# List tiles of a routed FFN: weights fetched per tile from DRAM into fixed buffers, the bias as one matmul, result addresses on VectorE

## The chip, the cores and the metric

One Trainium2 chip, one core of it. The metric is the device time of one execution in microseconds; a run's time is somewhat longer than the span that its profile covers. On this core TensorE (PE) multiplies, VectorE (DVE) and ScalarE (ACT) work on SBUF and PSUM, GpSimd (POOL) works on SBUF and issues indirect DMAs, and SyncE (SP) issues the plain ones.

## The reference

`x` is 4 batches of 512 tokens of width 128 (2048 tokens). Four residual blocks follow one another, each on a layer-normalised `x`: causal attention with 16 heads of 8 and rotary positions, a routed FFN, a gated scan with a convolution of three taps, and the same routed FFN again. The FFN, which the change is about, cut to its core:

```python
scores = sigmoid(xf @ Wg.T + bg + bias)                  # 8 experts
top_scores, top_idx = top_k(scores, 2)                   # two per token
weights = zeros(T, E).at[arange(T)[:, None], top_idx].add(top_scores)
h = gelu(einsum('td,ehd->teh', xf, W1) + b1)             # hidden 512
eo = einsum('teh,edh->ted', h, W2) + b2
combined = einsum('ted,te->td', eo, weights)
shared = gelu(xf @ Ws1.T + bs1) @ Ws2.T + bs2
out = shared + combined
```

## The kernel before

One program of five engine streams, ordered by hand: every stream is written out in its own order and they meet through semaphores. Attention takes the first 285 us, the FFN some 210 to 500, the scan and the second FFN's routing the stretch to 657, the second FFN's tiles the rest.

**Weights.** Each FFN weight is scaled and split into a high and a low float16 half during attention (`take_high_weights` on ScalarE, `take_low_weights` on VectorE, line 1441). `w1` and `w2` hold both halves of all eight experts and of the shared one, resident in SBUF. A product of two split numbers is three matmuls (`PRODUCTS`: high by high, low by high, high by low).

**Routing.** For each batch VectorE picks two experts per token and computes the row of each (token, expert) pair in that expert's list. GpSimd splits the token into halves (`split_rows`, L634 and L635) and scatters it to `rows_dram`, 128 rows a DMA, eight DMAs a batch (`scatter`, L643). In the first FFN GpSimd's order is: reciprocal root of the norm (L512), split, scatter of the batch before, and once, behind the first scatter, `bias_table` (L616 to L625). That one scales `b1` (24 rows of 512: three copies of the eight experts), splits it in three bfloat16 parts, and leaves in `bias_rows` part k on copy k. `map_tiles` on VectorE (L1593 to L1609) then tells for each of NT = 39 list tiles which expert it belongs to (`tile_expert`), which row it starts at (`tile_row`), and, in `which`, a column that picks the expert's three bias rows. The shared expert's matmuls (`shared_up` L1140, `shared_down` L1159) run over all tokens with fixed weight addresses.

**List tiles.** `tiles(r)` of each engine handles 39 tiles of 128 rows, 78 over both FFNs. TensorE's order is a loop of rounds: in round k it does `turn(k)`, `up(k - 1)` and `down(k - LAG)`, LAG = 3.

- SyncE: `tiles` waits for the map and the scatters, then per tile reads the row number into a register (L490) and loads 128 rows of 520 bytes to `xg` (L491), seven buffers.
- TensorE `turn`: two transposes (L1182). `up`: reads the tile's expert number into a register (L1186), four bias matmuls of 128 columns (L1189), twelve matmuls with `w1[:, w, expert, ...]` (L1194), whose addresses come from the register. `down`: twelve with `w2[:, w, expert, ...]` (L1205).
- VectorE: `turned` copies the transposed tile out of PSUM (L1636), `low` makes the hidden layer's low half (L1642), `results` copies the result (L1650).
- ScalarE: gelu (L831), then the high half (L836).
- GpSimd: `address` computes where each result row goes (L652, L654), `store` sends the tile to `y_dram` by an indirect DMA (L661).

PSUM's eight banks go round in the fixed order of `bank_order()`; `bank_full` and `bank_free` carry it, so waiting for `bank_full` of `("dn", r, s)` means waiting for the last down matmul of tile s. Behind the tiles SyncE gathers `y_dram` in batches of 512 KB (L497) and VectorE adds them to `x` (L1665).

Of the kernel before, what the change touches and what calls it, by code (L numbers as in the profile page):

```python
# [103 lines left out]
LAG = 3  # L104
S_AT = TILES_OF
# [4 lines left out]
PART_AT = MOD_AT + 1  # L110
# [67 lines left out]
def hybrid_block_kernel(nc, x_in, wqkv_in, wo_in, bo_in, w1_in, b1_in, w2_in, b2_in, wg_in, gate_rows_in,  # L178
# [3 lines left out]
    with ExitStack() as ctx:  # L182
# [39 lines left out]
        bias_rows = sb("bias_rows", [P, F], BF16)  # L222
# [97 lines left out]
        hid16 = part(arena, 2048, [2, C, L], F16)  # L320
        yg = part(arena, 4096, [2, TT, 2, D])
# [5 lines left out]
        bias_tmp = heads_arena[:, 2048:3072]  # L327
# [8 lines left out]
        bias_parts = k_words[:, 3 * L:4 * L].bitcast(BF16).rearrange("p (a f) -> p a f", a=2)  # L336
# [3 lines left out]
        b1e = rope_s[:].rearrange("p t d -> p (t d)")[0:3 * E, 0:F]  # L340
# [8 lines left out]
        rows_dram = [nc.dram_tensor(f"rows_dram{r}", [ROWS, ROW // 2], I32, kind="Internal") for r in range(FFNS)]  # L349
        y_dram = nc.dram_tensor("y_dram", [RESULTS, D], F32, kind="Internal")  # L350
# [38 lines left out]
        zeroed = sem("zeroed")  # L389
        post_step = sem("post_step")  # L390
# [66 lines left out]
        def _(sp):  # L457
# [22 lines left out]
            def tiles(r):  # L480
                sp.wait_ge(map_ready, r + 1)
                for b in range(B):
                    sp.wait_ge(scattered[b], 16 * 2 * TT * (r + 1))
                for s in range(NT):
# [24 lines left out]
        def _(pool):  # L509
# [99 lines left out]
            def bias_table():  # L609
# [3 lines left out]
                rows = slice(0, 3 * E)  # L613
                scaled, rest = (bias_tmp[rows, i * F:(i + 1) * F] for i in range(2))
# [31 lines left out]
            def tiles(r):  # L646
                def address(s):
                    n = r * NT + s
# [1211 lines left out]
```

## Time and profile before

| | us |
|---|---|
| median of 3 runs | 800.47 (799.57 to 800.96) |
| the profiled execution | 800.33 |
| its span | 798.5 |
| TensorE busy | 566.2 (71%) |
| VectorE, ScalarE, GpSimd busy | 466.9, 344.6, 327.8 |
| first row load of the tile stages | 376.05 and 658.12 |

The profile comes from one execution. An engine's busy time is the union of its instructions; a wait is put down to what ended last before it. "PEld" are TensorE's weight loads, "PEldq" and "SPq" the register and DMA instructions of a sequencer, "issue" is time for which nothing in the profile accounts. The tiles' buffers have the names of what they are cut from: `arena` is `hid_t`, `xgT`, `y_t` and `yg` (and, after the change, the weight buffers), `probs` is `hid16_t`, `qk_sb` is `xg`, `w` is `w1` or `w2`.

### The profile page before, as it was taken

What the parts mean: (1) busy time and instruction counts of PE and PEld (TensorE: products, weight loads), DVE (VectorE), ACT (ScalarE), POOL (GpSimd) and SP (SyncE); (2) the same over time, 40 slices, a digit from 0 to 9 for tenths busy, and PEclk for the clock granted to TensorE, in tenths of its full rate; (3) what the DMA queues carried; (4) which work ended last, traced back from release to release, by engine and by line L of the source; (5) the groups of instructions that cost most, each with busy time, mean ns of one, the idle gap of its engine ahead of it and who ended that gap; (6) DMA issues with size and microseconds to landing.
All of it is one profiled execution on the core that took longest, in us unless ns stands there. A gap on an engine that the chain in (4) does not pass through costs nothing. (4 is left out here: it accounts for less than half of the span.)

```text
span 798.5 us, 16946 instructions
## 1 busy us (share of the span) xinstructions
PE 566.2 (71%) x5836; PEld 377.7 (47%) x5836; DVE 466.9 (58%) x1241; ACT 344.6 (43%) x462; POOL 327.8 (41%) x447
## 2 busy tenths in 40 slices
PE   3488887888888744564888886545777667888870
PEld 2354554545544333342766665122424446666650
DVE  5868767676677354465433443488796763443434
ACT  0254645655665423452444443131524444444430
POOL 5036028018100027765466555112432544566550
PEclk9789999999999957687899999675958768999995
DMA  8999000000000010011211111200000002111105
GB/s 297 321 335 298 2 2 2 2 1 2 2 1 2 1 30 27 18 31 40 56 49 48 45 39 30 77 27 0 28 15 14 27 28 57 48 48 48 38 29 161
DMA packets 45146, 46.37 MB, mean 58 GB/s; under 512 B 5369, under 2 KB 42386, under 8 KB 44810
## 3 DMA queue, kind: packets, MB, share of 16 engines
q1 hardware_dynamic: 40522, 35.91, 15.0%
q0 software_dynamic: 4544, 9.38, 3.6%
q8 instruction: 52, 0.85, 0.5%
q14 instruction: 28, 0.23, 0.1%
HBM read 16.75 MB, written 28.52 MB: 57 GB/s over the span
## 5 line engine op out<-in xcount | busy, mean ns | idle before, releaser
L1384 DVE TENSOR_REDUCE row_maxima<-ps 128x2 f32<-128x256 f32 (+3 forms) x128 | 99.0, 817 | 44.1 <-PE ps L958 43.9
L661 POOL DMA_INDIRECT y_dram<-arena,goes_to x78 | 85.4, 1095 | 82.1 <-DVE arena L1650 73.9
L710 ACT ACTIVATE probs<-ps 128x768 f32<-128x768 f32 (+1 forms) x96 | 82.5, 884 | 81.1 <-PE ps L983 81.1
L831 ACT ACTIVATE arena<-ps,up_back 128x512 f32<-128x512 f32 x78 | 53.6, 688 | 133.5 <-PE ps L1194 133.5
L512 POOL TENSOR_TENSOR rstd<-var_eps,minus_half 128x4 f32<-128x4 f32 x16 | 17.0, 1061 | 220.5 <-DVE var_eps L1321 220.5
L1650 DVE COPY arena<-ps 128x128 f32<-128x128 f32 x78 | 22.8, 292 | 127.4 <-PE ps L1205 127.3
L643 POOL DMA_INDIRECT rows_dram<-probs,idx x64 | 68.9, 1077 | 49.4 <-DVE idx L1582 29.5
L1194 PE MATMUL ps<-arena,w 128*128 128x128 f16 x936 | 87.0, 227 | 0.2
L1205 PE MATMUL ps<-w,probs 128*128 x936 | 85.2, 217 | 1.2 <-DVE probs L1642 0.8
L1003 PE MATMUL ps<-probs,v_tok 128*16 128x256 f32 (+3 forms) x512 | 74.7, 434 | 2.5 <-ACT probs L710 2.5
L1205 PEld LDWEIGHTS ps<-w,probs 128*128 128x128 f16 x936 | 66.5, 96 | 15.9 <-issue 2.7
L1194 PEld LDWEIGHTS ps<-arena,w 128*128 x936 | 65.8, 99 | 12.0 <-issue 1.1
L1642 DVE SCALAR_TENSOR_TENSOR probs<-arena,hid_scale,probs 128x512 f16<-128x512 f32 x78 | 58.8, 753 | 4.2 <-ACT probs L836 3.8
L836 ACT ACTIVATE probs<-arena,hid_scale 128x512 f16<-128x512 f32 x78 | 56.3, 721 | 2.6
L1189 PE MATMUL ps<-which,bias_rows 128*128 128x128 bf16 x312 | 32.3, 227 | 30.7 <-issue 30.7
L1003 PEld LDWEIGHTS ps<-probs,v_tok 128*16 128x16 f32 x512 | 24.2, 96 | 47.7 <-issue 35.6
L953 PE MATMUL ps<-heads_arena 48*128 48x128 bf16 (+3 forms) x256 | 37.8, 310 | 11.6 <-DVE row_maxima L1384 6.3
L978 PE MATMUL ps<-q2T,heads_arena 50*128 50x512 bf16 (+3 forms) x256 | 38.5, 310 | 9.1 <-ACT probs L710 7.1
L1189 PEld LDWEIGHTS ps<-which,bias_rows 128*128 128x128 bf16 x312 | 18.7, 100 | 43.5 <-issue 43.5
L652 POOL TENSOR_SCALAR result_row<-qk_sb,list_end 128x1 f32<-128x1 f32 x78 | 30.4, 390 | 16.4 <-DMA qk_sb<-rows_dram 6.6
L958 PE MATMUL ps<-mask_qk,neg_eye 64*128 64x128 bf16 x512 | 35.1, 222 | 0.0
L1159 PE MATMUL ps<-w,arena 128*128 128x128 f16 x384 | 25.1, 226 | 12.8 <-DVE arena L1616 12.8
(234 smaller groups left out, 1091.3 us busy)
## 6 DMA issues: line engine op xcount, KB each, us to landing
rows_dram<-grids SPq DMA_DIRECT2D x2, 8840.0 KB, 43.7
qk_sb<-rows_dram SPq DMA_DIRECT2D x78, 65.0 KB, 1.8
arena<-in_w SPq DMA_DIRECT2D x2, 2304.0 KB
arena<-y_dram SPq DMA_DIRECT2D x8, 512.0 KB, 4.1
y_dram<-arena,goes_to POOLq DMA_INDIRECT x78, 2.4
x_all<-in_x SPq DMA_DIRECT2D x4, 256.0 KB, 8.1
rows_dram<-probs,idx POOLq DMA_INDIRECT x64, 2.3
out_x<-x_all SPq DMA_DIRECT2D x4, 256.0 KB, 3.7
```

The lines of the kernel that those rows point to most:

```text
L643: nc.gpsimd.indirect_dma_start(rows_dram[r].ap(), bass.IndirectOffsetOnAxis(ap=idx[:, r, b, t, k:k + 1], axis=0), xrow_words[:, b % 2, t, ...
L661: nc.gpsimd.indirect_dma_start(y_dram.ap(), bass.IndirectOffsetOnAxis(ap=goes_to[:, n % YT:n % YT + 1], axis=0), y_t[:, n % YT, :], None). ...
L710: nc.scalar.activation(probs[:, n % 2, :, PROB_AT[u]:PROB_AT[u] + size], ps[:, of:of + 2, 0:size], ACT.Exp).then_inc(slot_free[slot_of(("T ...
L831: nc.scalar.activation(hid_t[:, n % HT, :], ps[:, of, :], ACT.Gelu, scale=up_back[:]).then_inc(bank_free[of], 1)
L836: nc.scalar.activation(hid16_t[:, n % HT, 0, :], hid_t[:, n % HT, :], ACT.Identity, scale=hid_scale[:]).then_inc(high_t_ready, 1)
L978: pe.matmul(ps[:, to + h, o:o + size], kT[rows, a % 2, p, j * P:(j + 1) * P], q2T[rows, n % 2, j * P:L], start=True, stop=False)
L1003: mm = pe.matmul(ps[quadrant:quadrant + VW, PV_BANK, j * P:L], v_tok[:, a % 2, j, 2 * p + h, :], probs[:, n % 2, h, at:at + size], start=( ...
L1189: pe.matmul(ps[:, to, c * P:(c + 1) * P], bias_rows[:, c * P:(c + 1) * P], which[:, s:s + 1].broadcast_to([P, P]), start=(c == 0), stop=Fa ...
L1194: mm = pe.matmul(ps[:, to, c * P:(c + 1) * P], w1[:, w, bass.ds(expert[s], 1), c * P:(c + 1) * P].rearrange("p o f -> p (o f)"), xgT[:, (r ...
L1205: mm = pe.matmul(ps[:, to, 0:D], hid16_t[:, n % HT, v, c * P:(c + 1) * P], w2[:, w, bass.ds(expert[s], 1), c, :].rearrange("p o d -> p (o ...
L1384: ins = nc.vector.tensor_reduce(row_maxima[:, t, 2 * p:2 * p + 2], ps[:, of:of + 2, o:o + keys], AX.X, ALU.max)
L1642: nc.vector.scalar_tensor_tensor(hid16_t[:, n % HT, 1, :], hid_t[:, n % HT, :], hid_scale[:], hid16_t[:, n % HT, 0, :], ALU.mult, ALU.subt ...
```

## The change

Five things change. The weight halves are stored to a DRAM tensor once, during attention, by four DMAs on SyncE: for each expert 128 rows of 4096 bytes (both halves of `w1` and of `w2`). SyncE loads each tile's 512 KB of weights into one of WT = 4 buffers; the order of its loads is weights 0, rows 0, rows 1, then rows s and weights s - 1 by turns, and weights s waits for the down matmuls of tile s - 4. The first load of a stage waits for the last `shared_down`, as the buffers lie where `hid` and `hid16` are. TensorE's matmuls have fixed addresses, and `tile_expert` is gone. The bias table is 96 rows of 128 columns (each expert's four blocks of 128 become rows), and one matmul of 512 columns with a `which` of four columns a tile puts the bias in. The result addresses are computed on VectorE, in `turned`.

```diff
+WT = 4
+WROW = 4 * F
+BIAS_ROWS = 3 * E * C
...
-        which = sb("which", [P, NT], BF16)
-        tile_expert = sb("tile_expert", [P, NT], I32)
+        which = sb("which", [P, NT, C], BF16)
+        weight_row = sb("weight_row", [P, NT], I32)
...
+        wt = part(arena, 0, [WT, WROW], F16)
+        w1t, w2t = (wt[:, :, 2 * F * i:2 * F * (i + 1)].rearrange("p n (w f) -> p n w f", w=2) for i in range(2))
...
+        weights_dram = nc.dram_tensor("weights_dram", [X * P, WROW], F16, kind="Internal")
...
+            of_parts = weights_dram.ap().rearrange("(x p) (k w f) -> p k w x f", p=P, k=2, w=2)
+            sp.wait_ge(low_ready, 2 * PIECES)
+            for i, parts in enumerate((w1[:], w2[:].rearrange("p w x c d -> p w x (c d)"))):
+                for w in range(2):
+                    sp.dma_start(of_parts[:, i, w], parts[:, w]).then_inc(weights_stored, 16)
...
+                def load_weights(s):
+                    n = r * NT + s
+                    if s >= WT:
+                        before = ("dn", r, s - WT)
+                        sp.wait_ge(bank_full[bank_of(before)], count_of(before))
+                    row = sp.value_load(weight_row[0:1, s:s + 1], min_val=0, max_val=E * P)
+                    sp.dma_start(wt[:, n % WT, :], weights_dram.ap()[bass.ds(row, P), :]).then_inc(wt_loaded[n % WT], 16)
...
+                sp.wait_ge(map_ready, r + 1)
+                sp.wait_ge(weights_stored, 16 * 4)
+                sp.wait_ge(bank_full[bank_of(("sd", r, B - 1))], count_of(("sd", r, B - 1)))
+                load_weights(0)
+                for b in range(B):
+                    sp.wait_ge(scattered[b], 16 * 2 * TT * (r + 1))
+                for s in range(NT + 2):
+                    if s < NT:
+                        load_rows(s)
+                    if s >= 2 and s - 1 < NT:
+                        load_weights(s - 1)
...
-                rows = slice(0, 3 * E)
-                scaled, rest = (bias_tmp[rows, i * F:(i + 1) * F] for i in range(2))
+                rows = slice(0, BIAS_ROWS)
+                scaled, rest = (bias_tmp[rows, i * P:(i + 1) * P] for i in range(2))
...
                 def store(s):
                     n = r * NT + s
+                    pool.wait_ge(goes_to_ready, n + 1)
...
-                for k in range(NT + LAG):
-                    if k < NT:
-                        address(k)
-                    if k >= LAG:
-                        store(k - LAG)
+                for s in range(NT):
+                    store(s)
...
                 def up(s):
-                    expert[s] = pe.value_load(tile_expert[0:1, s:s + 1], min_val=0, max_val=E)
+                    n = r * NT + s
                     to = give2(("up", r, s))
-                    for c in range(C):
-                        pe.matmul(ps[:, to, c * P:(c + 1) * P], bias_rows[:, c * P:(c + 1) * P],
-                                  which[:, s:s + 1].broadcast_to([P, P]), start=(c == 0), stop=False, skip_group_check=True)
+                    pe.matmul(ps[:, to, :], bias_rows[0:BIAS_ROWS, :], which[0:BIAS_ROWS, s, :].unsqueeze(2).broadcast_to([BIAS_ROWS, C, P]),
+                              start=True, stop=False, skip_group_check=True)
+                    pe.wait_ge(wt_loaded[n % WT], 16 * (n // WT + 1))
                     read2(("tr", r, s))
...
-                                           w1[:, w, bass.ds(expert[s], 1), c * P:(c + 1) * P].rearrange("p o f -> p (o f)"),
+                            mm = pe.matmul(ps[:, to, c * P:(c + 1) * P], w1t[:, n % WT, w, c * P:(c + 1) * P], xgT[:, n % GT, v, :], start=False, stop=(v == 1), skip_group_check=True)
...
-                                           w2[:, w, bass.ds(expert[s], 1), c, :].rearrange("p o d -> p (o d)"),
+                                           w2t[:, n % WT, w, c * D:(c + 1) * D],
...
-                nc.vector.tensor_scalar(which[:], expert_of[:], grids[:, MOD_AT:MOD_AT + 1], None, ALU.is_equal)
-                nc.vector.tensor_copy(tile_expert[:], expert_of[:])
+                for c in range(C):
+                    nc.vector.tensor_scalar(which[:, :, c], expert_of[:], grids[:, MOD_AT + c:MOD_AT + c + 1], None, ALU.is_equal)
+                nc.vector.tensor_scalar(weight_row[:], expert_of[:], float(P), None, ALU.mult)
...
                 def turned(s):
                     n = r * NT + s
+                    dve.wait_ge(xg_loaded[n % XG], 16 * (n // XG + 1))
+                    nc.vector.scalar_tensor_tensor(result_row[:, n % YT:n % YT + 1], xg_words[:, n % XG, D:D + 1], list_end[:, s:s + 1],
+                                                   xg_words[:, n % XG, D + 1:D + 2], ALU.is_lt, ALU.add).then_inc(address_ready, 1)
...
+                    dve.wait_ge(address_ready, n + 1)
+                    if n >= YT:
+                        dve.wait_ge(y_stored[n % YT], 16 * (n // YT))
+                    nc.vector.tensor_scalar(goes_to[:, n % YT:n % YT + 1], result_row[:, n % YT:n % YT + 1],
+                                            grids[:, SPARE_AT + s:SPARE_AT + s + 1], None, ALU.max).then_inc(goes_to_ready, 1)
```

TensorE's program in one round of a tile stage, before: the transposes, the register load of `up`, and the first matmuls of `up`; `ISA` and `REGISTER_ALU` are register operations.

```order
L1205 REGISTER_ALU
L1205 MATMUL ps<-w,probs 128x128 x2
L1182 MATMUL ps<-ident_f,qk_sb 128x128 x2
L1186 TENSOR_LOAD tile_expert
L1186 ISA x2
L1189 MATMUL ps<-which,bias_rows 128x128 x4
L1194 ISA
L1194 MATMUL ps<-arena,w 128x128
L1194 ISA
L1194 MATMUL ps<-arena,w 128x128 x2
```

The same place after the change:

```order
L1199 MATMUL ps<-ident_f,qk_sb 128x128 [waits xg_loaded3,bank_free4]
L1199 MATMUL ps<-ident_f,qk_sb 128x128
L1205 MATMUL ps<-which,bias_rows 128x512 [waits bank_free5]
L1211 MATMUL ps<-arena 128x128 [waits bank_free1,wt_loaded1]
L1211 MATMUL ps<-arena 128x128 x11
L1220 MATMUL ps<-arena,probs 128x128 [waits low_t_ready,bank_free6]
L1220 MATMUL ps<-arena,probs 128x128 x11
```

The register load and the register operations are gone, and `up` waits for a `wt_loaded` behind its bias matmul. SyncE's queue in the steady part of a stage, before:

```order
L490 TENSOR_LOAD tile_row [waits bank_full2,goes_to_ready]
L490 ISA x2
L491 ISA
L491 DMA qk_sb<-rows_dram 128x130
L490 TENSOR_LOAD tile_row [waits bank_full3,goes_to_ready]
```

and after:

```order
L501 TENSOR_LOAD weight_row [waits bank_full4]
L501 ISA x2
L502 ISA
L502 DMA arena<-weights_dram 128x2048
L510 TENSOR_LOAD tile_row [waits bank_full6,goes_to_ready]
L510 ISA x2
L511 ISA
L511 DMA qk_sb<-rows_dram 128x130
L501 TENSOR_LOAD weight_row [waits bank_full7]
```

A weight load stands between two row loads, behind a wait of its own.

## Rows read from the trace of the kernel before

**Rows 1.** The page: busy shares; 40 slices of TensorE, of DMA traffic

```profile
...
PE 566.2 (71%) x5836; PEld 377.7 (47%) x5836; DVE 466.9 (58%) x1241; ACT 344.6 (43%) x462; POOL 327.8 (41%) x447
...
PE   3488887888888744564888886545777667888870
...
GB/s 297 321 335 298 2 2 2 2 1 2 2 1 2 1 30 27 18 31 40 56 49 48 45 39 30 77 27 0 28 15 14 27 28 57 48 48 48 38 29 161
...
```

**Rows 2.** Busy time by stretch: us, busy (instructions) by engine, granted clock, DMA share, GB/s

```profile
...
673.00:767.00 94.00, 80.66 (x965) 63.87 (x964) 38.33 (x96) 45.27 (x65) 57.83 (x97) 1.00 0.16 44
369.20:372.00 2.80, 2.80 (x49) 2.70 (x49) 1.03 (x1) 0.00 (x0) 2.19 (x3) 1.00 0.14 48
...
```

**Rows 3.** Groups of 673 to 767: line engine op xcount | busy us, mean ns | idle before

```profile
...
L661 POOL DMA_INDIRECT y_dram<-arena,goes_to x33 | 36.0, 1090 | 32.4 <-DVE arena L1650 27.5 <-issue 3.0 <-POOL goes_to L654 1.8
...
L654 POOL TENSOR_SCALAR goes_to<-result_row,grids 128x1 int32<-128x1 f32 x32 | 9.7, 303 | 3.0
L1650 DVE COPY arena<-ps 128x128 f32<-128x128 f32 x32 | 9.3, 292 | 55.4 <-PE ps L1205 55.4
...
```

**Rows 4.** The chain of waits, 694 to 702: start us, us, what

```profile
...
697.67 0.38 issue
698.06 0.40 PE ps L1189 x4
698.46 0.92 PE ps L1194 x12
699.38 1.02 PE ps L1205 x12
...
```

**Rows 5.** Instructions of line 1186, then of line 1205, sequencer: min/median/max ns

```profile
...
L1186 PEldq TENSOR_LOAD <-tile_expert x78: 296/301/492, 379.2 to 770.4; - x78
...
...
L1205 PEldq ALU_OP  x624: 32/32/42, 385.1 to 775.6; - x156
...
```

**Rows 6.** Timeline of TensorE, shared_down of the last batch: start us, us

```profile
...
369.18 2.84 PE L1159 MATMUL ps<-w,arena 128*128 128x128 f16 x48 [3.29 <-DVE arena L1616]
...
```

**Rows 7.** Timeline of GpSimd and VectorE around the bias table

```profile
...
289.24 0.61 POOL L634 CAST probs<-heads_arena 128x512 f16<-128x512 f32 x1 [1.22 <-DVE heads_arena L1327]
...
312.38 0.68 POOL L616 TENSOR_SCALAR heads_arena<-rope_s,up_scale 24x512 f32<-24x512 f32 x1
...
313.13 0.61 POOL L617 CAST k_tok<-heads_arena 24x512 bf16<-24x512 f32 x1
...
324.46 1.04 POOL L512 TENSOR_TENSOR rstd<-var_eps,minus_half 128x4 f32<-128x4 f32 x1
325.63 1.12 DVE L1327 TENSOR_SCALAR heads_arena<-x_all,mean,rstd 128x128 f32<-128x128 f32 x4 [12.37 <-POOL rstd L512]
...
```

**Rows 8.** The chain of waits, 654 to 664, where the second stage starts

```profile
...
654.90 2.29 DMA rows_dram<-probs,idx
...
658.12 0.35 SPq L491
...
659.30 1.84 DMA qk_sb<-rows_dram
...
661.27 0.37 PE ps L1182 x2
...
```

**Rows 9.** The page, DMA issues: KB each, median us to landing

```profile
...
qk_sb<-rows_dram SPq DMA_DIRECT2D x78, 65.0 KB, 1.8
...
arena<-y_dram SPq DMA_DIRECT2D x8, 512.0 KB, 4.1
...
```

**Rows 10.** Busy time by stretch: the loads of w1 and w2; the end of attention

```profile
...
12.00:19.00 7.00, 5.06 (x14) 3.67 (x15) 1.89 (x2) 0.59 (x1) 3.70 (x8) 1.00 1.00 424
250.00:285.00 35.00, 26.40 (x308) 14.40 (x302) 15.77 (x35) 16.65 (x23) 0.00 (x0) 0.96 0.00 1
...
```

**Rows 11.** Timeline of VectorE, the tile map of the second FFN

```profile
...
649.64 0.24 DVE L1607 TENSOR_SCALAR which<-expert_of,grids 128x39 bf16<-128x39 f32 x1
...
```

**Rows 12.** Timeline of VectorE, the last low half of a weight

```profile
...
251.96 0.81 DVE L1441 SCALAR_TENSOR_TENSOR w<-arena,down_scale,w 128x576 f16<-128x576 f32 x1
...
```

More of the change, by code:

```diff
@@ L109 @@
 MOD_AT = ONES_AT + E
-PART_AT = MOD_AT + 1
+PART_AT = MOD_AT + C
 TOK_AT = PART_AT + 3
@@ L221, in hybrid_block_kernel @@
         x_all = sb("x_all", [P, B, TT, D])
-        bias_rows = sb("bias_rows", [P, F], BF16)
+        bias_rows = sb("bias_rows", [P, P], BF16)
         grids = sb("grids", [P, GRIDS])
@@ L389, in hybrid_block_kernel @@
         zeroed = sem("zeroed")
+        weights_stored = sem("weights_stored")
+        wt_loaded = [sem(f"wt_loaded{i}") for i in range(WT)]
+        address_ready = sem("address_ready")
         post_step = sem("post_step")
@@ L480, in tiles, with load_rows @@
             def tiles(r):
[L481 to L484, printed above, removed]
+                def load_weights(s):
[5 more added lines that the diff above has]
+                    sp.dma_start(wt[:, n % WT, :], weights_dram.ap()[bass.ds(row, P), :]).then_inc(wt_loaded[n % WT], 16)
+                def load_rows(s):
                     n = r * NT + s
@@ L646, in tiles @@
             def tiles(r):
-                def address(s):
-                    n = r * NT + s
-                    pool.wait_ge(xg_loaded[n % XG], 16 * (n // XG + 1))
-                    if n >= YT:
-                        pool.wait_ge(y_stored[n % YT], 16 * (n // YT))
-                    link(nc.gpsimd.tensor_scalar(result_row[:, n % YT:n % YT + 1], xg_words[:, n % XG, D:D + 1], list_end[:, s:s + 1],
-                                                 xg_words[:, n % XG, D + 1:D + 2], ALU.is_lt, ALU.add))
-                    nc.gpsimd.tensor_scalar(goes_to[:, n % YT:n % YT + 1], result_row[:, n % YT:n % YT + 1],
-                                            grids[:, SPARE_AT + s:SPARE_AT + s + 1], None, ALU.max).then_inc(goes_to_ready, 1)
-                    pool.wait_ge(goes_to_ready, n + 1)
                 def store(s):
                     n = r * NT + s
+                    pool.wait_ge(goes_to_ready, n + 1)
                     pool.wait_ge(bank_free[bank_of(("dn", r, s))], count_of(("dn", r, s)))
@@ L1173, in tiles @@
                 pe.wait_ge(bias_ready, 1)
-                expert = {}
                 def turn(s):
@@ L1193, in up @@
                         for w, v in PRODUCTS:
-                            mm = pe.matmul(ps[:, to, c * P:(c + 1) * P],
-                                           w1[:, w, bass.ds(expert[s], 1), c * P:(c + 1) * P].rearrange("p o f -> p (o f)"),
-                                           xgT[:, (r * NT + s) % GT, v, :], start=False, stop=(v == 1), skip_group_check=True)
+                            mm = pe.matmul(ps[:, to, c * P:(c + 1) * P], w1t[:, n % WT, w, c * P:(c + 1) * P], xgT[:, n % GT, v, :], start=False, stop=(v == 1), skip_group_check=True)
                     full(("up", r, s), mm)
@@ L1805, in shape_constants @@
     grids[:, ONES_AT:ONES_AT + E] = 1.0
-    grids[:, MOD_AT] = np.where(rows < 3 * E, rows % E, -1)
-    grids[:, PART_AT:PART_AT + 3] = rows[:, None] // E == np.arange(3)[None, :]
+    for c in range(C):
+        grids[:, MOD_AT + c] = np.where((rows < BIAS_ROWS) & (rows % C == c), rows // C % E, -1)
+    grids[:, PART_AT:PART_AT + 3] = rows[:, None] // (E * C) == np.arange(3)[None, :]
     grids[:, TOK_AT:TOK_AT + B * TT] = SPARE + 2 * (rows[:, None] + P * np.arange(B * TT))
@@ L1846 @@
         "wout": a["L0_attn_b_W_out"].T.reshape(2, P, D).transpose(1, 0, 2),
-        "b1e": np.tile(a["L0_ffn_b1"], (3, 1)),
+        "b1e": np.tile(a["L0_ffn_b1"].reshape(E * C, P), (3, 1)),
         **shape_constants(),
```

7 lines of the change are left out of this document (3 added, 4 removed).

## The prediction

> **What bounds the kernel now.** I read the page's shares first: TensorE is busy 71% of the span, the DMA engines little after the first tenth, and slices 19 to 23 and 33 to 38, the two list-tile stages, are TensorE's at 8 tenths [rows 1]. The cut of 94 us from the second stage (busy time by stretch) gives the same at full clock, 2.4 GHz [rows 2]; the groups of that stretch count 32 copies of line 1650, one a tile [rows 3], so a tile takes 94 / 32 = 2.94 us. The chain of waits runs through nothing but TensorE there, and its pieces repeat: two transposes, 0.38 us of "issue", four bias matmuls 0.40, twelve of line 1194 0.92, twelve of line 1205 1.02 [rows 4]. The issue piece is the register load of the expert number, 0.30 us and what follows it [rows 5]. Eight register operations stand among the twelve matmuls of either line (line 1205's are 624 for 78 tiles) [rows 5]. They cost more than they look: 48 matmuls of the same shape with fixed addresses took 2.84 us, granted clock 1.00 [rows 2, 6], so with 0.22 for the last one's own length they start (2.84 - 0.22) / 47 = 0.056 us apart, where line 1194 needs 0.92 / 12 = 0.077 and line 1205 1.02 / 12 = 0.085.
>
> In the same stretch VectorE is busy 38.3 / 32 = 1.20 us a tile, ScalarE 1.41, GpSimd 1.81 [rows 2]. None of them bounds the stage.
>
> Ahead of the first stage another engine rules. GpSimd runs the scatters one behind the other and then the ten operations of the bias table, from 312.38 to 324.46, and VectorE waits 12.37 us for the reciprocal root that is queued behind them [rows 7].
>
> **TensorE's share of a tile.** The change takes off the register load (0.38) and all sixteen register operations. Twenty-four matmuls at 0.056 are 1.34 us instead of 1.94. The bias becomes one matmul of 512 columns, as many columns as four of 128: 4 x 0.056 = 0.22 instead of 0.40. With two transposes (0.11) TensorE's own work is 1.34 + 0.22 + 0.11 = 1.67 us, against 2.94. Were that the whole change, the stages would shrink by 1.27 us a tile, 99 us in all. It isn't, since the matmuls now wait for 512 KB of weights each.
>
> **What takes its place: the turn of a weight buffer.** Four buffers are shared by tiles s, s-4, and so on. SyncE can issue the load of tile s only after the down matmuls of tile s-4, the last work of round s-1; up(s) wants it in round s+1, behind the transposes and the bias. From the end of down(s-4) to the end of down(s-2), which is two rounds, the chain is:
> - SyncE from signal to DMA: the scatter lands at 654.90 + 2.29 = 657.19 and the first row load is issued at 658.12 [rows 8], 0.93, which holds three waits where one will stand: 0.8.
> - The transfer. A row load of 65 KB lands 1.8 us after issue [rows 9]. The 447 KB more go at what 18 KB rows got, 424 GB/s [rows 10]: 458 thousand bytes / 424 = 1.1. Store of results: it starts on the same signal and moves another 64 KB through the same engines, 0.15 to 0.2. Together 3.1.
> - Landing to matmul: 661.14 to 661.27 [rows 8], 0.13.
> - up(s) and down(s-2): 1.34, and 0.16 until the last one has drained (its 0.22 less a step of 0.056).
>
> Sum 5.5, so a round takes 2.75 us. That is above TensorE's 1.67, VectorE's and ScalarE's load, and SyncE's own: two loads a round at (659.30 - 658.12) = 1.18 each [rows 8] are 2.36. A tile gains 2.94 - 2.75 = 0.19. The first four tiles gain nothing: weights 3 are the eighth load in SyncE's order, there 7 x 1.18 + 0.8 + 3.1 + 0.1 = 12.3 us after its start, where before 4.1 us to the second transposes [rows 8] and somewhat under three rounds had gone. Some 35 rounds are left in each stage: 35 x 0.19 x 2 = **13.3 us off**.
>
> Between ends: the nearest row of the same size is the gather of 512 KB, 4.1 us to landing [rows 9], but in 1 KB pieces where a weight row is 4 KB. It gives (0.8 + 4.1 + 0.13 + 1.50) / 2 = 3.27. The other end: DMA is busy 0.16 x 2.94 = 0.47 us a tile now, for rows and results together [rows 2]; if all of that were the row load's short pieces, and nothing collided, a transfer would take 1.8 - 0.47 + 524 / 424 = 2.6, a round 2.5, and SyncE's 2.36 is the floor. I take 3.1, nearer to the row load, because the path (SyncE, 128 whole rows out of DRAM) is the same. The Trainium skill, "DMA: Bandwidth & Descriptors", section "Anatomy of one DMA — SWDGE (gpsimd) path", has a fit for GpSimd's path of about 2.0 us plus bytes over 436e9 a second; by it 512 KB would land in 3.2 and a round would take 2.80, where the gather's row would give 3.27. No row here shows a load in 4 KB pieces.
>
> **The bias table.** 24 x 512 becomes 96 x 128. A cast of 128 x 512 took 0.61 and one of 24 x 512 0.61 [rows 7], so only columns count. The ten operations take 12.1 us, of which ten gaps of some 0.08 (313.06 to 313.13 is the first) leave 11.3 busy. If everything scales with columns 8.5 go. If each keeps 0.3 us, the length of a 128x1 operation [rows 3], it's 11.3 - (3.0 + 8.3 / 4) = 6.2. I take **6.5 us off**, all of it on the path: VectorE, TensorE and ScalarE all wait there for the root behind it, and GpSimd is queued solid from there to the stage's end.
>
> **Smaller edits.** The tile map gains three operations of 128x39, 0.24 each [rows 11] but begun before the last has ended, which delays the last shared_down by some 0.4, and SyncE's first weight load (1.18) waits for that: it ends some 0.4 after the scatters have landed. That is 0.5 a stage, **1 us on**. The result addresses leave GpSimd, which keeps a store of 1.09 a tile [rows 3]; VectorE gets two operations of one column (0.30 on GpSimd, taken as no more here) and stays under 1.8 of 2.75: nothing, unless rounds fell below 1.8. The weights go to DRAM once, 4.7 MB in four DMAs: the last low half is made at 252.0 [rows 12] and the DMA engines are idle until 285 [rows 10]. At the 300 GB/s of the page's first slices [rows 1] they take 16 us, so they are over before the late loads: nothing. If it weren't covered it would hold those loads, and so TensorE, by up to 16.
>
> Sum against the profiled execution, 800.3 (span 798.5 and 1.8 around it, median 800.5): 800.3 - 13.3 - 6.5 + 1.0 = 781.5, rounded to **781**.
>
> **The rivals.**
> 1. *Loads land sooner, and SyncE's queue binds.* Transfer 2.6 us or less, round 2.5 down to 2.36. For it: 424 GB/s was reached [rows 10], and the DMA engines have room [rows 2]. Against: stores and loads start together. 70 x 0.44 = 31 to 70 x 0.58 = 41 off, with the table and the smaller edits 764 to 754.
> 2. *Slower: the buffer's turn is too long.* The load lands like the gather, 4.1 us. Round 3.27, 70 x 0.33 = 23 on, less 5.5: 818. It turns from gain to loss where 70 x (T - 2.94) = 5.5, T = 3.02, a transfer of 3.6 us. For it: the same size took 4.1. Against: four times as many pieces, and another read beside it.
> 3. *TensorE falls to 1.2 GHz.* Each round now has about 1.1 us of standing still. At half clock matmuls are twice 0.056 apart, its own work 30 x 0.112 = 3.4 and a round (0.8 + 3.1 + 0.13 + 2.69 + 0.3) / 2 = 3.5: 70 x 0.56 = 39 on, less 5.5: 834. Against: the granted clock was 1.00 [rows 2] with (30 x 0.056) / 2.94 = 57% of the time streaming, and it would be 61% now. [...]
> 4. *The register operations aren't what spaces the matmuls.* Then up and down keep 1.94: round (0.8 + 3.1 + 0.13 + 1.94 + 0.16) / 2 = 3.07, 9 on, less 5.5: 804. The shared matmuls' 0.056 [rows 6] speaks against it.
>
> **How the numbers follow.** Forecast (round 2.6 to 2.95, 771 to 796): 0.55. Rival 1: 0.23. Rival 2: 0.12. Rival 3: 0.06. Rival 4: 0.04. About 0.2% (1.6 us) is what a measurement can tell from no change. Rounds near 3.0 leave 0.04 for "same"; rivals 2 to 4 are slower, less the part that falls short of 3.02: 0.15; faster is 0.81. The range reaches from rival 1's floor to rounds of 3.1, half of the way to rival 2: 755 to 806.
>
> **What would show it.** Line 1194's and 1205's successors start 0.056 apart; no register load on TensorE; TensorE idle about 1.1 us a tile, ended by a DMA of arena<-weights_dram; that DMA at 3.1 us to landing (under 2.6: rival 1, then SyncE never waits; over 3.6: rival 2); granted clock 1.00 (rival 3: below). The bias table takes about 5.6 us, and scatters end 6.5 earlier. I am wrong at the root if TensorE's idle time ends with VectorE or GpSimd.

## Result and profile after

The changed kernel takes **812.11 us** (median of 4 runs, 809.57 to 813.71); the kernel before, measured beside it, 800.72 (4 runs, 799.57 to 801.51). The ratio is 1.014, 95% interval 1.011 to 1.017: **slower, by some 11 us**. I had forecast 781, faster, in a range that ends at 806. The profiled executions are 809.57 us (span 807.8) against 800.33 (span 798.5), so the traces have to account for 9.3 us. Of all the runs below one, an execution of run 3, took 1234.36 us beside 814.03 to 822.94 for the others, and it is left out of that run's figures.

The page of the changed kernel (shares, slices of TensorE, granted clock, DMA and its traffic, then DMA issues in KB and median us to landing), against [rows 1, 9]:

```profile
PE 523.8 (65%) x5602; PEld 346.3 (43%) x5602; DVE 491.9 (61%) x1403; ACT 344.4 (43%) x462; POOL 281.8 (35%) x291
...
PE   3488887888888654667566563457766646666650
...
PEclk9789999999999957786999998665876777999995
DMA  8999000000004210014766674100000026777655
GB/s 295 325 335 282 2 2 2 2 1 2 2 1 147 90 30 26 28 44 135 227 199 220 208 225 128 40 13 14 14 27 1 28 67 204 217 220 227 206 161 159
...
arena<-weights_dram SPq DMA_DIRECT2D x78, 512.0 KB, 3.7
...
qk_sb<-rows_dram SPq DMA_DIRECT2D x78, 65.0 KB, 2.9
...
arena<-y_dram SPq DMA_DIRECT2D x8, 512.0 KB, 4.1
y_dram<-arena,goes_to POOLq DMA_INDIRECT x78, 3.8
...
```

TensorE has lost 42 us of work (566.2 to 523.8) and still the span is longer. In both list-tile stages (slices 19 to 23 and 33 to 38) it has gone from 8 tenths to 5 or 6, and the traffic from 48 to some 215 GB/s. The weights land 3.7 us after issue, and the row loads beside them have gone from 1.8 to 2.9.

Busy time from 673 to 767, then the groups of that stretch by line (busy us, mean ns | idle before, and what ended it), against [rows 2, 3]:

```profile
673.00:767.00 94.00, 58.76 (x839) 47.76 (x837) 46.45 (x155) 43.67 (x62) 39.33 (x31) 0.99 0.70 213
```

```profile
L683 POOL DMA_INDIRECT y_dram<-arena,goes_to x31 | 39.5, 1276 | 70.4 <-DVE goes_to L1660 61.3 <-DVE arena L1674 8.8 <-issue 0.3
...
L1211 PE MATMUL ps<-arena 128*128 128x128 f16 x372 | 26.4, 221 | 33.7 <-DMA arena<-weights_dram 33.7
...
L1205 PE MATMUL ps<-which,bias_rows 96*128 96x512 bf16 x31 | 12.1, 389 | 0.0
L1674 DVE COPY arena<-ps 128x128 f32<-128x128 f32 x31 | 9.0, 292 | 45.1 <-PE ps L1220 45.1
...
```

In the same 94 us 31 tiles pass (31 bias matmuls, 31 result copies of line 1674) where 32 did before, so a tile takes 3.03. TensorE stands still for 33.7 us in that stretch ahead of its up matmuls, 1.09 a tile, all of it ended by a weight load; row loads end another 1.6 us. VectorE, ScalarE and GpSimd are busy for half of it or less.

The chain of waits from 699 to 711 shows the turn of a buffer twice over (start us, us, what). Against [rows 4] the links are the prediction's: up matmuls, down matmuls, SyncE, transfer.

```profile
699.12 3.79 DMA arena<-weights_dram
702.91 0.05 issue
702.96 0.84 PE ps L1211 x12
703.80 0.69 PE ps L1220 x12
...
704.50 0.29 SPq L501
...
705.23 3.28 DMA arena<-weights_dram
...
708.56 0.84 PE ps L1211 x12
709.40 0.69 PE ps L1220 x12
...
710.81 3.77 DMA arena<-weights_dram
```

From one issue of this chain to the next it is 6.11 us and then 5.58, and each of these spans two rounds. The median over the 68 loads of both stages after their first five: 0.74 from the last down matmul's end to the issue (the prediction took 0.8), 3.74 from the issue to the first up matmul (3.1 + 0.13; it is 3.69 to the landing and 0.05 from there), 1.5 for the matmuls. Two rounds are thus 6.0, one 3.0; counted from first up matmul to first up matmul, tiles 5 to 38, the rounds average 3.07 in the first stage and 3.01 in the second, against 2.92 and 2.93 before.

The changed kernel's account, both profiled executions set beside each other at the same events:

| event | change against before, us |
|---|---|
| first row load of stage 1 (376.05, now 370.29) | -5.75 |
| stage 1, from that load to the last down matmul (118.22, now 124.85) | +6.62 |
| from there to the second stage's last eight scatters | +0.1 |
| second stage's start, from the first of these scatters to the first row load | +2.4 |
| stage 2 (117.85, now 123.63) | +5.78 |
| the tail | +0.1 |
| sum | +9.3 |

The -5.75 is mostly the bias table. GpSimd's timeline of it, against [rows 7]:

```profile
312.25 0.37 POOL L648 TENSOR_SCALAR heads_arena<-rope_s,up_scale 96x128 f32<-96x128 f32 x1
312.69 0.29 POOL L649 CAST k_tok<-heads_arena 96x128 bf16<-96x128 f32 x1
...
317.50 1.04 POOL L544 TENSOR_TENSOR rstd<-var_eps,minus_half 128x4 f32<-128x4 f32 x1
```

The root starts at 317.50 where it started at 324.46, 7.0 us sooner. The cast fell from 0.61 to 0.29.

Most of the +2.4 is a collision. The chain where the second stage starts, against [rows 8]:

```profile
656.35 4.21 DMA rows_dram<-probs,idx
...
661.48 0.36 SPq L511
...
662.66 1.86 DMA qk_sb<-rows_dram
```

SyncE issues the first weight load at 656.47, just after the last scatter has started, and that scatter lands after 4.21 us instead of 2.29, 1.9 of the 2.4. The rest is GpSimd's: the fifth of the last eight scatters takes it 2.06 us instead of 1.62, as it also does in run 4, which has the longer tile map and no weight load. Run 7 has the same collision with a load of half the size, and there the scatter lands after 3.42. It is a matter of timing, though: in the same kernel's profiled execution on another chip (run 9) the first weight load is issued 2.57 us after the last scatter's start instead of 0.12, and the first row load comes 3.89 us after that start instead of 5.12 (before: 3.22). The ratio was the same there, so the collision is not what made the change a loss.

### The profile page after: what moved, and what is told of

Same layout as the page of the kernel before. It is cut to its first block and busy times, and to the rows that moved or that the text cites. A ratio compares the mean times of both kernels' runs of the same rounds, so it can differ in the third digit from the quotient of the medians.

```text
span 807.8 us, 15557 instructions
## 1 busy us (share of the span) xinstructions
PE 523.8 (65%) x5602; PEld 346.3 (43%) x5602; DVE 491.9 (61%) x1403; ACT 344.4 (43%) x462; POOL 281.8 (35%) x291
## 5 line engine op out<-in xcount | busy, mean ns | idle before, releaser
L683 POOL DMA_INDIRECT y_dram<-arena,goes_to x78 | 100.1, 1283 | 160.5 <-DVE goes_to L1660 140.7
L1211 PE MATMUL ps<-arena 128*128 128x128 f16 x936 | 70.5, 229 | 83.6 <-DMA arena<-weights_dram 83.5
L1211 PEld LDWEIGHTS ps<-arena 128*128 128x128 f16 x936 | 57.0, 102 | 110.5 <-DMA arena<-weights_dram 109.3
L1220 PE MATMUL ps<-arena,probs 128*128 128x128 f16 x936 | 66.2, 222 | 2.1 <-DVE probs L1666 2.1
L1220 PEld LDWEIGHTS ps<-arena,probs 128*128 128x128 f16 x936 | 56.9, 100 | 2.4 <-issue 2.4
L1158 PE MATMUL ps<-heads_arena,w 128*128 128x512 f16 x96 | 33.6, 524 | 0.0
L1001 PE MATMUL ps<-mask_kq,neg_eye 64*128 64x128 bf16 x512 | 33.1, 221 | 0.0
L1199 PE MATMUL ps<-ident_f,qk_sb 128*128 128x128 f16 x156 | 22.5, 229 | 14.3 <-DMA qk_sb<-rows_dram 14.2
```

What stands on the lines that cost most here:

```text
L683: nc.gpsimd.indirect_dma_start(y_dram.ap(), bass.IndirectOffsetOnAxis(ap=goes_to[:, n % YT:n % YT + 1], axis=0), y_t[:, n % YT, :], None). ...
L1211: mm = pe.matmul(ps[:, to, c * P:(c + 1) * P], w1t[:, n % WT, w, c * P:(c + 1) * P], xgT[:, n % GT, v, :], start=False, stop=(v == 1), ski ...
L1220: mm = pe.matmul(ps[:, to, 0:D], hid16_t[:, n % HT, v, c * P:(c + 1) * P], w2t[:, n % WT, w, c * D:(c + 1) * D], start=(c == 0 and k == 0) ...
```

## The experiments

Twelve runs, of which those of one group share a chip and its runs of the kernel before, whose median is 805.65 us for the first four, 801.99 for the next four, 808.54 for the last. The theory at this point, A where an expectation calls it so: the turn of a weight buffer (wait for the down matmuls, SyncE's issue, landing, up and down matmuls) sets the round, as the prediction had it, and what was mis-sized is the landing, 3.7 for 3.1. Its rivals are named with each run: that the bytes or the queues bind whatever the number of buffers, that VectorE's new operations do, or that the gains on TensorE never existed. A "round" is one tile's turn in TensorE's loop. The per-round figures are taken as above.

### 1. Six buffers

```
-WT = 4
+WT = 6
```

> The changed kernel with six weight buffers instead of four (WT = 6; the two more lie where the gathered results lie between stages). Theory A, the turn of a buffer: a round of the changed kernel is half of 0.74 us (signal to issue) + 3.75 (issue to first matmul) + 1.5 (up and down) = 3.0, and the transfer is long for reasons of its own (pieces of 0.16 to 0.55 us), not for want of DMA engines. With six buffers the same chain has four rounds to fit in (1.5 each) and no longer binds; next is SyncE, two loads a round at 1.16 to 1.18, 2.36. So rounds of 2.4 to 2.5, 70 rounds x 0.55 = 39 us less than 812: 765 to 780. Theory B, the DMA engines are the bound: with two loads in flight each lands later (5 us and more), rounds stay at 2.9 or over, time at 802 or over.

Measured: 764.76 us, ratio **0.949** (0.946 to 0.953). Rounds 2.30 and 2.31. The loads take longer (4.8 from issue to matmul, they overlap now), and yet the round is 0.7 shorter: the time was in the turn, not in the bytes as such. SyncE's stretch from one row load's register read to the weight load's landing, in the chain of waits:

```profile
689.81 0.26 SPq L510
...
690.39 0.29 SPq L511
...
690.93 0.33 SPq L501
...
691.29 0.15 SPq L501
...
691.70 5.13 DMA arena<-weights_dram
```

With four buffers SyncE issued each load 0.74 us after the down matmuls it had waited for, the register work behind that wait; here it is 2.99 behind them. SyncE no longer waits for a buffer, it is itself late: the two loads of a round take it 2.3 us, which the prediction had as a floor of 2.36 in its rival 1.

### 2. The register read ahead of the wait

```
+row = sp.value_load(weight_row[0:1, s:s + 1], min_val=0, max_val=E * P)
 if s >= WT:
     before = ("dn", r, s - WT)
     sp.wait_ge(bank_full[bank_of(before)], count_of(before))
-row = sp.value_load(weight_row[0:1, s:s + 1], min_val=0, max_val=E * P)
```

> The changed kernel with one line moved: SyncE reads the weight row into its register before it waits for the down matmuls, so that only the DMA itself is left behind the wait. Four buffers as before. Theory A: from the end of down(s-4) to the issue 0.74 becomes about 0.25, a round loses half of that, 0.25 us, 70 rounds x 0.25 = 17 us: 795 (791 to 799). Theory B (DMA engines bind): the landing grows by what the issue gains, 808 to 812.

Measured: 804.44 us, ratio 0.998 (0.996 to 1.000), rounds 2.90 and 2.92. Against the changed kernel's ratio of 1.014 that is some 13 us less, where I had expected 17 and named 795. The signal-to-issue time fell from 0.74 to 0.17 as meant, but the time to the matmul rose from 3.74 to 4.02. So 0.57 was taken out of two rounds and 0.28 came back: the landing is not a constant. That the turn is the bound stands (taking time out of it helps). Why the landing grew is argued only: a load that starts sooner runs more of its way beside the store and the row load of the round.

### 3. The first weight load behind the scatters

```
-load_weights(0)
 for b in range(B):
     sp.wait_ge(scattered[b], 16 * 2 * TT * (r + 1))
...
     load_rows(s)
+if s == 0:
+    load_weights(0)
```

> The changed kernel with the first weight load of a stage issued behind the first row load, after the wait for the scatters. In the changed kernel's second stage the last scatter took 4.2 us to land beside that load (2.3 in the kernel before), and the first row load came 2.4 us later than the shift of the work before it explains. If the collision is the cause, the last scatter lands in 2.3 again and the second stage's first row load comes some 2 us earlier (counted from the last scatter); the first up then waits for its weights, issued 1.2 later than the rows, so 1.2 of it is given back in each stage: 812 less 0 to 2. If the collision is not the cause, the scatter still takes about 4 us and the time is 812 to 815.

Measured: 820.65 us, ratio 1.014 (1.008 to 1.020), no better than the changed kernel. Its chain at the start of the second stage:

```profile
666.51 2.28 DMA rows_dram<-probs,idx
```

The scatter lands in 2.28 again, so the collision is real where the two start together. Moving the load does not win it back: the first up matmul now comes 5.6 us after the first row load instead of 3.8, for it waits for weights that were issued later. That such a scatter is held up by the weight load is shown by this run and the changed kernel's; that this cost anything which another place of the load would save is not, and by run 9 there is often nothing to save.

### 4. The new bias alone

The kernel before with the bias table of 96 x 128, `which` of four columns a tile, and the one bias matmul:

```
-for c in range(C):
-    pe.matmul(ps[:, to, c * P:(c + 1) * P], bias_rows[:, c * P:(c + 1) * P], which[:, s:s + 1].broadcast_to([P, P]), ...)
+pe.matmul(ps[:, to, :], bias_rows[0:BIAS_ROWS, :], which[0:BIAS_ROWS, s, :].unsqueeze(2).broadcast_to([BIAS_ROWS, C, P]), ...)
```

> The kernel before with the bias part of the change alone: table of 96 x 128, which of four columns, one matmul of 512 columns a tile. Weights, registers and addresses stay. If the parts add up: the table takes 6 us off the first FFN's routing, the single matmul takes 0.16 to 0.18 off each of 76 rounds of 2.94, 12 to 14 us: 781 (779 to 784). Rival: the sequencer's register operations set TensorE's pace there and the four short matmuls ran in their shadow, so only the table counts: 794 to 795.

Measured: 800.52 us, ratio **0.992** (0.990 to 0.995), which is 6.3 us of 805.65 (4.3 to 8.4). Rounds stay at 2.92. The chain of waits shows why the one matmul gives nothing (against [rows 4], where four of them took 0.40):

```profile
699.24 0.39 issue
699.63 0.39 PE ps L1189
700.02 0.95 PE ps L1194 x12
700.97 1.07 PE ps L1205 x12
```

One matmul fills the same 0.39. What ends that piece is the start of the first up matmul, and runs 5 and 6 below speak for the register work ahead of it as what comes late.

### 5 and 6. Fixed addresses; and no register read

Both start from the kernel before. Expert 0 is used for every tile, so the choice of expert is left out; the second also leaves out TensorE's register read.

```
-w1[:, w, bass.ds(expert[s], 1), c * P:(c + 1) * P].rearrange("p o f -> p (o f)")
+w1[:, w, 0, c * P:(c + 1) * P]
-w2[:, w, bass.ds(expert[s], 1), c, :].rearrange("p o d -> p (o d)")
+w2[:, w, 0, c, :]
```

```
-expert[s] = pe.value_load(tile_expert[0:1, s:s + 1], min_val=0, max_val=E)
```

> The kernel before, with the address of every list tile's weights fixed to expert 0: the choice of expert is left out of the computation, the register read of each tile stays, the 24 register-computed addresses of a tile go. If register work between the matmuls is what spaces them (the prediction's first step), the twelve up matmuls and the twelve down matmuls come at 0.056 us as in the changed kernel, TensorE's round falls from 2.92 by 12 x 0.021 + 12 x 0.029 = 0.6 us to about 2.3 to 2.4, and the kernel takes about 760 to 770. If it is something else that both kernels' list tiles share, the spacing stays at 0.077 and 0.085 and the time at 805. If GpSimd or SyncE binds at once, the spacing falls but the round stays near 2.9 and the time near 800.

> As the one with fixed addresses, and TensorE's register read of each tile is gone too (its SP-side reads stay). If the read of 0.30 us lies on TensorE's path, the round falls by another 0.2 to 0.3 us to about 2.1, and the time by some 20 us more; if TensorE waits for others by then (GpSimd's four instructions of a tile, 1.8 us, or the landing of the rows), the round stays where it was without the addresses.

Measured: 771.78 us, ratio **0.963** (0.961 to 0.965), and 767.85, ratio 0.959 (0.957 to 0.961). The timeline of TensorE without the read:

```profile
653.21 0.28 PE L1182 MATMUL ps<-ident_f,qk_sb 128*128 128x128 f16 x2
653.32 0.39 PE L1188 MATMUL ps<-which,bias_rows 128*128 128x128 bf16 x4
653.55 0.83 PE L1193 MATMUL ps<-arena,w 128*128 128x128 f16 x12
...
654.22 0.83 PE L1204 MATMUL ps<-w,probs 128*128 128x128 f16 x12
654.89 0.28 PE L1182 MATMUL ps<-ident_f,qk_sb 128*128 128x128 f16 x2
```

From transposes to transposes 1.68 us, and twelve matmuls from start to start 0.67, which is 0.056 each. The prediction had 1.67 for TensorE's own work. In both runs the rounds from the fourth to the thirteenth are 1.68, in the first with the register read still there. So the read costs nothing by itself: it was on the path only because the sequencer was behind with the addresses. After some thirteen tiles the lead is used up, and the chain of the one without the read is GpSimd's:

```profile
701.36 1.07 POOL y_dram L661
...
702.48 0.44 POOL result_row L652
...
703.01 0.29 POOL goes_to L654
...
703.68 1.07 POOL y_dram L661
```

One store to the next is 2.32 us, and the rounds of the whole stages average 2.32 and 2.28 with the read, 2.22 and 2.27 without. So GpSimd, busy 1.81 a tile before [rows 2], needs 2.3 with its waits and gaps, and would have bound the kernel before at once, had only its registers been mended.

### 7. Half a weight row

The changed kernel, 2 KB of each partition's 4 KB; the second weight matrix is left out, and the down matmuls multiply by the first.

```
-sp.dma_start(wt[:, n % WT, :], weights_dram.ap()[bass.ds(row, P), :])
+sp.dma_start(wt[:, n % WT, 0:2 * F], weights_dram.ap()[bass.ds(row, P), 0:2 * F])
-w2t[:, n % WT, w, c * D:(c + 1) * D]
+w1t[:, n % WT, w, c * D:(c + 1) * D]
```

> The changed kernel, each tile loading only the first half of its weight rows (2 KB of 4 KB in a partition, the down matmuls multiply by the same bytes as the up matmuls, so the second weight matrix is left out). Two buffer turns still share a load's whole way from TensorE's last down matmul to the first up matmul: 0.74 + landing + 1.5 us for two rounds. If the landing of 3.75 is mostly bytes (2.3 us of it are the time in which the 128 pieces run, eight a DMA engine), it falls to about 2.6, the round by 0.55 to 2.5, and the kernel to about 770. If it is mostly a fixed way of issue and completion, it falls by 0.3 at most, the round to 2.9, and the kernel to about 805. In between, with the first piece of each engine at 0.55 whatever its size and the other seven at half of 0.21: landing 3.0, round 2.7, kernel 785.

Measured: 772.53 us, ratio **0.965** (0.962 to 0.967), rounds 2.55 and 2.58. From its page, DMA issues:

```profile
arena<-weights_dram SPq DMA_DIRECT2D x78, 256.0 KB, 2.7
...
qk_sb<-rows_dram SPq DMA_DIRECT2D x78, 65.0 KB, 2.3
```

256 KB less make the landing 1.0 us shorter, which is 262 thousand bytes a us, 262 GB/s, where the prediction let the additional bytes go at 424. Mostly bytes, then, or the length of the pieces, which was halved with them; the number of pieces, 128, was not. Through both medians goes 1.7 us + bytes / 262 GB/s, which gives 2.0 at 65 KB, where the kernel before shows 1.8 [rows 9].

### 8. Addresses back on GpSimd

In the changed kernel both operations of a tile go from VectorE to GpSimd, to their old place three tiles ahead of the store:

```
+link(nc.gpsimd.tensor_scalar(result_row[...], xg_words[...], list_end[:, s:s + 1], ..., ALU.is_lt, ALU.add))
+nc.gpsimd.tensor_scalar(goes_to[...], result_row[...], grids[...], None, ALU.max).then_inc(goes_to_ready, 1)
...
-nc.vector.scalar_tensor_tensor(result_row[...], ...).then_inc(address_ready, 1)
-nc.vector.tensor_scalar(goes_to[...], ...).then_inc(goes_to_ready, 1)
```

> The changed kernel, with the two address operations of a tile back on GpSimd in their old place. By the theory of the buffer's turn neither VectorE nor GpSimd is on the path of a round: the round stays at 3.0 to 3.1 and the ratio to the kernel before at 1.010 to 1.018. If the operations on VectorE cost the round something (they stand behind its copies of the row tiles and its low halves), the round falls by up to their 0.4 us and the kernel by up to 30.

Measured: 813.09 us, ratio 1.017 (1.012 to 1.021), rounds 3.04 and 3.15. No change against the changed kernel: neither engine is on the path there.

### 9. The changed kernel again

> The changed kernel itself once more, on the chip of the runs beside it, so that they have it to stand against: ratio to the kernel before 1.010 to 1.017 if the first comparison holds on another chip too.

Measured: 819.45 us, ratio 1.016 (1.012 to 1.020), rounds 3.06 and 3.12. The result holds on another chip.

### 10. Five buffers

```
-WT = 4
+WT = 5
```

> The changed kernel with five weight buffers instead of four. By the theory of the turn, three rounds instead of two now share its 6.0 us, which is 2.0 a round, under the 2.3 that SyncE's two loads take: so five buffers do what six did, round 2.30, ratio to the kernel before 0.945 to 0.955. If the gain of six came from something that grows with each buffer (how far ahead the first loads run, or loads that spread over a longer time), five stand half way, at round 2.6 and ratio 0.98.

Measured: 774.22 us, ratio **0.961** (0.957 to 0.965), rounds 2.46 and 2.53: neither figure of mine. What I had left out is what run 1 had already shown: overlapping loads land later. The mean time from issue to matmul is 4.86 here against 3.81 with four buffers, the mean wait before it 1.04, and (1.04 + 4.86 + 1.5) / 3 = 2.47. It is still the turn, with three rounds to share it.

### 11 and 12. Six buffers without bounds tests; and with the early register read

```
-row = sp.value_load(weight_row[0:1, s:s + 1], min_val=0, max_val=E * P)
+row = nc.s_assert_within(sp.value_load(weight_row[0:1, s:s + 1]), 0, E * P, skip_runtime_bounds_check_because="...")
```

and the same for `tile_row`. Both values are bounded by how they are made: `weight_row` is P times a count of at most E; `tile_row` is at most 16384 + (39 - 32) x 128 = 17280, which is `ROWS - P`.

> Six weight buffers, and SyncE's two register reads of a round no longer test their bounds (the two instructions and their gaps are 0.26 us of the 1.17 that a load takes there; both values stay within bounds by how the tile map makes them). If SyncE binds at 2.30, a round falls by up to 0.52. What comes next is the DMA engines: busy 0.68 of 3.04 us in the changed kernel, which is 2.07 us a tile. So round 2.1, ratio to the kernel before about 0.93, some 14 us under six buffers alone. If SyncE is not what binds with six buffers, the round stays at 2.30 and the ratio at 0.949.

> As the one before it, and each weight load's register is read ahead of its wait. With six buffers SyncE does not wait for the buffer any more, so this changes nothing: within 0.2% of the one before it. If it is faster by over 0.3%, the buffer's wait still counts in some rounds.

Measured: 739.94 us, ratio **0.916** (0.911 to 0.920), rounds 2.02 and 2.10; with the early read 737.55 us, ratio **0.914** (0.911 to 0.916), rounds 1.97 and 2.03. The two can't be told apart, as expected. The rounds came out as I had expected, near 2.1. By the ratios the gain of dropping the tests is 27 us, where I had allowed 14; the two profiled executions are 19.5 apart (760.03 and 740.58, on two chips), and the two stages together are 20.5 shorter. The 2.07 us of DMA time a tile that I had taken for a floor was not quite one: the last kernel's rounds are 1.97 and 2.03, with the engines busy for 0.96 of them. Busy time of the last kernel by stretch:

```profile
640.00:700.00 60.00, 52.81 (x802) 45.77 (x799) 40.85 (x150) 39.73 (x59) 30.65 (x30) 1.00 0.96 321
```

Thirty tiles in 60 us, the DMA engines busy 0.96 at 321 GB/s, TensorE 0.88. So the DMA engines come next, by their share; no run takes bytes off this kernel to prove it. This is the fastest of the kernels tried, 71 us under the kernel before on its chip. With the same 577 KB loaded a tile, one more buffer after another and a lighter SyncE turn the changed kernel from 1.016 into 0.914.

## Why the prediction was wrong

**The step that failed** is the second link of the buffer's turn: "The transfer. A row load of 65 KB lands 1.8 us after issue [rows 9]. The 447 KB more go at what 18 KB rows got, 424 GB/s [rows 10]", together 3.1. The load lands in 3.7. The half load puts the bytes at 262 GB/s: 458 thousand bytes / 262 = 1.75, and 1.8 + 1.75 + 0.15 for the store is 3.7. The 424 came from a stretch in which large loads were queued behind each other and the DMA engines were busy 1.00 [rows 10]. A single load that is waited for doesn't get that rate: in the trace its 128 pieces of 4 KB take 2.35 us from the first one's start to the last one's end, after 0.97 us in which none runs, and the landing is seen 0.35 us behind them. Company is the smaller part of it: the first load of the first stage, issued at 369.03 with two row loads behind it and no store, took 3.43 to land, against 2.9 for it alone by the prediction's numbers. Put 3.7 in the prediction's own sum and it is (0.8 + 3.7 + 0.13 + 1.34 + 0.16) / 2 = 3.07, what the first stage shows; with the two small links as measured too (0.74 and 0.05) it is 3.0.

The kernel before had rows that warn, and I passed them by. In its DMA issues (KB, median us to landing):

```profile
wqkv<-in_wqkv SPq DMA_DIRECT2D x1, 192.0 KB, 2.9
...
bo<-in_bo SPq DMA_DIRECT2D x1, 64.0 KB, 2.1
```

Both are SyncE's and single, and 128 KB more took 0.8 us more, at 164 GB/s, though among other loads at the start. With the gather's 4.1 [rows 9] three rows spoke for slow bytes and one for fast. Rival 2, slower, was this case, and its point of decision, 3.6 us of transfer, agrees with what came; 0.12 was too small a chance for it. The prediction's range, rounds up to 3.1, did hold the measured rounds. What took the time out of it is what I had priced at nothing or little, the first tiles of a stage and the starts of both.

**The sum, term by term** (before to after; a stage counts from its first row load, its first three rounds and its last tile stand apart):

| term | forecast, us | traces, us |
|---|---|---|
| first three rounds after the stage's start, both stages | 0 | +1.3 +2.5 |
| rounds 4 to 38, both stages | -13.3 | +6.1 +3.9 |
| last tile, both stages | 0 | -0.7 -0.6 |
| bias table, up to the first row load of stage 1 | -6.5 | -5.8 |
| second stage's start, tile map | +1.0 | +2.5 |
| tail | 0 | +0.1 |
| sum | -18.8 | +9.3 |

**Point by point.**
- What bounds before, and register work among the matmuls: right. Runs 5 and 6 put the spacing at 0.056 and TensorE's own work at 1.68 (forecast 1.67), and rival 4 is out.
- The register load as 0.38 on the path: right in the sum, wrong as a cause. Without the addresses a round with the read is 1.68 as one without it (runs 5 and 6).
- The single bias matmul (0.40 to 0.22): TensorE's round without register work is 1.68 with four bias matmuls too, so four never cost more than one.
- The turn of a buffer: right, by runs 1, 2, 7 and 10. It was the thing to look for, and with 3.1 in it the answer still came out with the wrong sign.
- Row loads and stores beside the weights: the prediction gave them 0.15 to 0.2 and let the row load keep its 1.8. It lands in 2.9 and the store in 3.8. Stores end none of TensorE's idle time, and row loads 1.6 us of it in the 94.
- The bias table, 6.5 forecast: 7.0 on GpSimd, 6.3 (4.3 to 8.4) in run 4, which has the whole new bias.
- Addresses on VectorE, nothing: right (run 8). The weights stored to DRAM once: nothing, right; 9.1 us each, at 252.9 to 256.8, under attention.
- Smaller edits, 1 us on: too small at both starts. The first stage starts 5.75 sooner where the table gave 7.0, so 1.2 was lost there: 0.4 on GpSimd's scatters (the longest takes 2.17 us, 1.76 before) and 0.8 between the last scatter and the first row load, with SyncE still at its first weight load when the scatters have landed. At the second it was 2.4, with the collision that I had not asked about, and 1.1 in run 9, without it.
- First rounds: the fourth up matmuls start 12.3 and 13.2 us after the first row load, against 11.0 and 10.7. The prediction counted 12.3 for them and took it for what had gone before, but only 11 had.
- Rival 3, the clock: not as a state of the stage. The granted clock is 0.99 from 673 to 767, the 2.4 GHz level, although TensorE stands still for 1.1 us of every round. At the stage's start it is low for longer, as busy time by stretch shows (the clock is the third number from the end):

```profile
665.00:680.00 15.00, 11.25 (x111) 9.00 (x109) 6.07 (x20) 6.14 (x9) 2.49 (x2) 0.66 0.64 192
```

Before, the same stretch had 1.00. At 0.66 TensorE was at 1.2 GHz for two thirds of it. Counted from the first row load, the 2.4 GHz level comes after 11.3 and 13.6 us, against 8.7 and 6.6 before. The loop that the Trainium skill, "TensorE: Matmul & The Clock Gate", section "HAM oscillation — how this bites in real kernels", shows going cold on every pass waits for its DMA longer than its matmuls run. In the rounds here the wait is 1.09 us and the matmuls are busy for 1.9, so they are another case, and the trace has them at 0.99.

On the transfer: by the fit of the Trainium skill, "DMA: Bandwidth & Descriptors", section "Anatomy of one DMA — SWDGE (gpsimd) path", an estimate for this load is 3.2 (it is for GpSimd's path, and this is SyncE's), which in the prediction's sum is a round of 2.82, not 2.80. The trace has 3.7, and the trace decides.

**Still open:** how much of a stage's slow start is TensorE at 1.2 GHz and how much the late weights. Part of it can be read off: on the chain of waits of the second stage the up and down matmuls from 671.49 on take 2.75 us at 1.2 GHz, where they take 1.5 later, so 1.2 us of that start is the clock's. The rest no run separates. Open, too, is by what way a weight load holds up a scatter that has already begun, and how much of the landing's 3.7 is the store and the row load beside it.

## What to carry to other kernels

When resident data becomes a load for each tile, write down the turn of a buffer (release, issue, landing, use) and divide it by the number of rounds that the buffers give it; if the margin to the round of today is smaller than the uncertainty of the landing time, add buffers before anything else, since here one more buffer was worth 5.5% (0.961 against 1.016) and two 6.6%. Take the landing time from a transfer that is waited for, alone, in the same size, not from the throughput of a full queue. And count the issuing engine's time for each load: behind the turn stood SyncE with 1.15 us a load, and behind SyncE, by their busy share of 0.96, the DMA engines.

## What the runs showed of the hardware

- Register-computed addresses among matmuls: 0.077 to 0.085 us from matmul to matmul instead of 0.056, and 30 us of the kernel's 802 (run 5).
- A SyncE load with an address from a register takes 1.15 us of that engine. The bounds test in it takes 0.15 us and its gaps: without the two tests of a round, six buffers went from rounds of 2.31 to 2.06.
- A load of 512 KB in 4 KB pieces lands after 3.7 us, one of 256 KB in 2 KB pieces after 2.7. Of the first's 128 pieces about ten take over 0.35 us, 0.7 on average, half of them within 0.3 us of the first one's start; most of the others take 0.16.
- Loads that overlap slow each other: 3.8 us from issue to matmul with four buffers, 4.9 with five, 4.8 with six, 5.3 with six and a lighter SyncE.
- One matmul of 512 columns takes 0.39 us, and four of 128 take 0.39 from the first one's start to the last one's end (changed kernel, run 6).
- A scatter that shared its start with a 512 KB load (issued 0.12 us later) landed in 4.21 us instead of 2.28, and beside one of 256 KB (run 7) in 3.42.
